# An adaLN block with fast weights and experts: own places for the rows of expert blocks, and another order of the engines at the boundary between two chunks of the scan

## The reference

```python
h = LN(x) * (1 + ca) + sa
x = x + ga * attn(h)            # test-time training with fast weights
h = LN(x) * (1 + cb) + sb
x = x + gb * ffn(h)             # top 2 of 8 experts, with LoRA
```

```python
gate, hb = ki @ w0, ki @ w2;  sg = silu(gate);  hidden = sg * hb
dh = vi @ w1.T;  dhbm = dh * sg;  dgba = silu_backprop(dh * hb, gate)
w1 += NS(einsum(hidden * lr1, vi));  w0 += NS(einsum(ki * lr0, dgba));  w2 += NS(einsum(ki * lr2, dhbm))
w = w / (norm(w) + 1e-5) * norm(w at the start)     # each of the three
o = (silu(qi @ w0) * (qi @ w2)) @ w1
```

## Time and profile before

| | before |
|---|---|
| median of 3 runs | 896.85 us (895.22 to 898.75) |
| profiled execution | 899.54 us, span 897.8 us |
| PE busy | 833.9 us, 93% |
| DVE busy | 687.4 us, 77% |
| ACT busy | 649.2 us, 72% |
| POOL busy | 350.4 us, 39% |
| mean granted clock | 0.984 |

### The profile page before, as it was taken

The page is one execution under the profiler, slowest core; times in us unless marked ns, Lnnn a source line. Parts: engine busy times, 40 slices in busy tenths (PEclk is TensorE's granted clock), DMA queues, the critical chain, the costliest instruction groups (busy, mean ns, idle before and its releaser), DMA issues.

```text
span 897.8 us, 16374 instructions
## 1 busy us (share of the span) xinstructions
PE 833.9 (93%) x4972; PEld 514.8 (57%) x4972; DVE 687.4 (77%) x2354; ACT 649.2 (72%) x1417; POOL 350.4 (39%) x324
## 2 busy tenths in 40 slices
PE   6999999999999999999999999998799999999994
PEld 3647576675757667575766757575555444444441
DVE  2798989898898989889898988989686554454441
ACT  2878988888888889889898988987485434444441
POOL 2324344444544444453444445344114232222222
PEclk9999999999999999999999999999899999999998
DMA  9776435161633517154251614438615465555450
GB/s 326 270 223 178 111 103 154 62 199 46 180 102 112 149 64 213 51 163 109 81 140 51 189 44 100 107 119 251 181 28 93 79 127 93 94 95 86 79 92 4
DMA packets 79126, 111.01 MB, mean 124 GB/s; under 512 B 14128, under 2 KB 35760, under 8 KB 78400
## 3 DMA queue, kind: packets, MB, share of 16 engines
q1 hardware_dynamic: 70720, 92.85, 36.7%
q0 software_dynamic: 8176, 16.85, 9.9%
q10 hardware_dynamic: 144, 0.26, 0.1%
HBM read 47.22 MB, written 64.55 MB: 124 GB/s over the span
## 4 chain that ended last, share of the span: by engine, by line
PE 63%; DVE 15%; ACT 8%; DMA 6%; issue 4%; POOL 3%; SPq 0%; DVEq 0%; POOLq 0%; ACTq 0%
PE bank L129 17%; PE bank L135 7%; PE bank L1060 7%; DMA out_x<-t_arena,t_tokx 4%; PE bank L1070 4%; POOL t_small L2871 2%; PE bank L613 2%; DVE t_small L1549 2%; PE bank L709 2%; ACT t_arena L2481 2%; PE bank L650 1%; PE bank L618 1%; PE bank L645 1%; PE bank L636 1%; DMA xs_scratch<-t_arena 1%
## 5 line engine op out<-in xcount | busy, mean ns | idle before, releaser
L129 PEld LDWEIGHTS bank<-t_arena 128*128 128x128 bf16 (+1 forms) x1536 | 123.2, 122 | 111.4 <-issue 30.5
L129 PE MATMUL bank<-t_arena 128*128 128x128 bf16 (+1 forms) x1536 | 156.1, 236 | 13.0 <-ACT t_arena L2490 6.4
L1060 PE MATMUL bank<-t_arena 128*128 x208 | 93.6, 593 | 0.0
L135 PE MATMUL bank<-t_ident,t_arena 128*128 128x128 f32 x398 | 65.5, 280 | 11.7 <-DVE t_arena L1105 6.2
L3027 POOL DMA_INDIRECT out_x<-t_arena,t_tokx x25 | 38.8, 1552 | 93.7 <-DMA out_x<-t_arena,t_tokx 77.3
L135 PEld LDWEIGHTS bank<-t_ident,t_arena 128*128 128x128 f32 x398 | 46.1, 142 | 45.6 <-issue 17.3
L2798 ACT ACTIVATE t_arena<-t_arena,t_small 128x128 f32<-128x128 f32 x100 | 41.1, 481 | 35.4 <-DVE t_tokx L2191 35.4
L2877 POOL TENSOR_TENSOR t_small<-t_small,t_half 128x8 f32<-128x8 f32 x14 | 24.5, 1748 | 103.5 <-DVE t_small L1549 103.5
L1060 PEld LDWEIGHTS bank<-t_arena 128*128 128x128 f32 x208 | 37.5, 190 | 37.3 <-issue 37.3
L129 PE MATMUL bank<-t_W,t_arena 128*128 128x128 f32 x384 | 54.8, 288 | 0.6 <-ACT t_W L2389 0.2
L1070 PE MATMUL bank<-t_arena 128*128 x108 | 50.8, 593 | 0.5 <-ACT t_arena L2793 0.5
(11 more groups left out here) (1121 smaller groups left out, 2406.9 us busy)
## 6 DMA issues: line engine op xcount, KB each, us to landing
xs_scratch<-t_arena SPq DMA_DIRECT2D x16, 2064.0 KB
t_arena<-xs_scratch SPq DMA_DIRECT2D x156, 64.0 KB
t_arena<-in_gate_up SPq DMA_DIRECT2D x32, 256.0 KB, 3.9
wm_scratch<-t_arena SPq DMA_DIRECT2D x30, 256.0 KB
t_arena<-in_wmod SPq DMA_DIRECT2D x5, 1024.0 KB, 10.4
t_arena<-in_down SPq DMA_DIRECT2D x16, 256.0 KB, 3.1
out_x<-t_arena SPq DMA_DIRECT2D x16, 256.0 KB, 2.1
t_arena<-wm_scratch SPq DMA_DIRECT2D x4, 1024.0 KB
```

Source lines behind the costliest of these rows:

```text
L129: mm = pe.matmul(bank[:, s], lhs[:, s], rhs[:, s], start=True, stop=True)
L135: mm = pe.transpose(bank[:, 128 * k:128 * k + 128], src[:, 128 * k:128 * k + 128], idn)
L1060: mm = pe.matmul(AA(u)[:, :], xT[u % 2][:, 128 * k:128 * k + 128], w_e[:, bass.ds(which[u], 1), 512 * k:512 * k + 512], start=(k == 0), st ...
```

## The change

Two parts in one kernel.

**A, the boundary.** On PE, raw1, raw2, raw0 are turned into B0, B2, B1, the expert-weight matmuls (step `mg`, still L709 in the new numbering) stand ahead of the logits, of raw0's transposes and of the turning of W, which goes W2, W0, W1; the rank matmuls stand behind all of them. On DVE the router's steps from lgc to msk stand behind the scaling of WT1; the merges of chunk c are in the next pass: u0 behind bn_aggr, u1 behind dgb, u2 behind the cast of n2's norm. On ACT kl0 stands between tg and the copy of hb, vl between tm and the cast of G2, both in the next pass; the copies of W go W2, W0, W1. PE has two new waits for merges (u1 before the first matmul into P1, u2 before the first into P2). Chunks 0 and 14 are changed in the same way.

**B, the rows.** Every block's rows, weight and token numbers have a place of their own among 29 (the later blocks take the places of the first again), each block a semaphore `s_g[b]` of its own; `mark` and `s_is` are gone.

```diff
@@ PE, chunk c
                 mm.then_inc(rate_pe, 1)
+                pe.wait_ge(mg_dve, nth(MG_DVE, p-2, "u1"))
                 pe.matmul(P1[:, :], hT[p % 2][:, 0:128], wqkv[1][:, 0, :], start=True, stop=False)
...
+                pe.wait_ge(mg_dve, nth(MG_DVE, p-2, "u2"))
                 pe.matmul(P2[:, :], hT[p % 2][:, 0:128], wqkv[0][:, 0, :], start=True, stop=False)
...
-                turned(pe, P1, raw[1], 4, ident[:, :]).then_inc(prep_pe, 1)
+                pe.wait_ge(n0_act, nth(N0_ACT, c, "ZT1"))
+                turned(pe, B0, raw[1], 4, ident[:, :]).then_inc(prep_pe, 1)
...
-                turned(pe, P2, raw[2], 4, ident[:, :]).then_inc(prep_pe, 1)
...
-                turned(pe, P0, raw[0], 4, ident[:, :]).then_inc(prep_pe, 1)
-                pe.wait_ge(prep_act, nth(PREP_ACT, min(c + 1, NC - 1), "kT"))
-                pe.wait_ge(prep_act, nth(PREP_ACT, min(c + 1, NC - 1), "qT"))
+                pe.wait_ge(n2_act, nth(N2_ACT, c, "ZT1"))
+                turned(pe, B2, raw[2], 4, ident[:, :]).then_inc(prep_pe, 1)
+                pe.wait_ge(mg_dve, nth(MG_DVE, c-1, "u0"))
                 pe.wait_ge(mg_dve, nth(MG_DVE, c-1, "u2"))
                 for j, (e, k) in enumerate(UNITS[c]):
...
                 mm.then_inc(mg_pe, 1)
+                pe.wait_ge(apply_act, nth(APPLY_ACT, a, "lgT"))
+                pe.matmul(A0[:, 0:NE], lgT[:, :], selr[:, 0:NE], start=True, stop=True).then_inc(apply_pe, 1)
...
+                turned(pe, B1, raw[0], 4, ident[:, :]).then_inc(prep_pe, 1)
+                pe.wait_ge(n2_dve, nth(N2_DVE, c, "WT"))
+                pe.wait_ge(prep_act, nth(PREP_ACT, p, "vT"))
+                turned(pe, B2, WT[2], 4, ident[:, :]).then_inc(n2_pe, 1)
                 pe.wait_ge(n0_dve, nth(N0_DVE, c, "WT"))
+                pe.wait_ge(prep_act, nth(PREP_ACT, p, "kT"))
                 turned(pe, B0, WT[0], 4, ident[:, :]).then_inc(n0_pe, 1)
-                pe.wait_ge(n2_dve, nth(N2_DVE, c, "WT"))
-                turned(pe, B2, WT[2], 4, ident[:, :]).then_inc(n2_pe, 1)
+                pe.wait_ge(n1_dve, nth(N1_DVE, c, "WT"))
+                pe.wait_ge(prep_act, nth(PREP_ACT, p, "qT"))
+                turned(pe, B1, WT[1], 4, ident[:, :]).then_inc(n1_pe, 1)
                 pe.wait_ge(apply_dve, nth(APPLY_DVE, a, "msk"))
...
@@ SP, reads of the blocks' rows
-            sp.wait_ge(s_sa, 16)
-            sp.wait_ge(s_is, 2)
-            at = sp.value_load(row0u[0:1, 6:6 + 1], min_val=0, max_val=2048 * NE - 128)
-            rows_in(sp, 6, at)
...
+            for t in range(NB):
+                if t == RING + 4:
+                    store_x1(NC - 2)
...
+                if t >= SLOTS:
+                    sp.wait_ge(s_sa, 16 * (t - SLOTS + 1))
+                at = sp.value_load(row0u[0:1, t:t + 1], min_val=0, max_val=2048 * NE - 128)
+                rows_in(sp, t, at)
```

More of the change, by code:

```diff
@@ L250, in adaln_block @@
         xT = cut(26624, 512, 2)
-        mark = arena[0:1, 28160:28160 + NB]
         def AA(u):
@@ L2383, in _ @@
             row.then_inc(prep_act, 1)
-            for h in range(H):
-                s = slice(128 * h, 128 * h + 128)
-                row = act.activation(kl0[1][:, s], raw[1][:, s], ACT.Identity, scale=lr12[1][:, 0 + h:1 + h])
-            row.then_inc(prep_act, 1)
             act.wait_ge(n0_pe, nth(N0_PE, 0, "TW"))
@@ L2565, in _ @@
             act.activation(tg, B0[:, :], ACT.Tanh, scale=0.5).then_inc(fwd_act, 1)
+            act.wait_ge(rate_dve, nth(RATE_DVE, NC - 1, "lr"))
+            act.wait_ge(prep_dve, nth(PREP_DVE, NC - 1, "tk"))
+            act.wait_ge(n0_pe, nth(N0_PE, NC - 3, "G"))
+            for h in range(H):
+                s = slice(128 * h, 128 * h + 128)
+                row = act.activation(kl0[1][:, s], raw[1][:, s], ACT.Identity, scale=lr12[1][:, 0 + h:1 + h])
+            row.then_inc(prep_act, 1)
             act.wait_ge(fwd_pe, nth(FWD_PE, NC - 1, "hb"))
```

432 lines of the change are left out of this document (192 added, 240 removed).

## The result

The changed kernel took 918.62 us (median of 4 runs, 917.91 to 920.77) against 896.84 us for the kernel before: the ratio is 1.0253, with a 95% interval of 1.0233 to 1.0274. It is slower by 21.8 us.

The account below looks back on a forecast made before the run. PE, busy for 93% of the span, bounds the kernel. 13 periods at +1.50 give 19.5, with +0.8 and +1.2 at the scan's ends and -1.45 at the tail +20.05 us, so 917.0 us; range 898 to 923.

Parts of the forecast that it names:

- The removed wait: PE's 0.90 us wait for qT's copy ahead of L709 goes; gate at best 0.27 us earlier a boundary.
- the copies of W ... are early enough: ACT at the boundary: copies in order W2, W0, W1, without kl0, come early enough for the 0.27 us gain.
- The rank wait: Rank matmuls directly ahead of the gate wait for DVE's msk: gate 0.54 us later (bounds -0.27 to +0.84).
- The reading of the Trainium skill's page: DVE's six router steps go at the pitch of independent operations, so the gate would gain 0.27 us; the prediction doubted it.
- kl0: On ACT, kl0 ahead of the copy of hb delays G2: 0.47 us a chunk (bounds 0 to 1.18).
- The merges: u0, u1, u2 in DVE's dense stretch of the next chunk: +0.49 us a chunk (bounds 0 to 1.83).
- 0.49 more than at G2: PE at the rate matmuls behind n1's norm sum: some 1.50 us late, 0.49 more than G2's 1.01.
- The period: One chunk of the scan: 39.05 + 0.54 + 0.47 + 0.49 = 40.55 us, +1.50.
- Rival 4: PE's boundary waits bring four or five more chunks with a lowered clock, adding 5 to 6 us: 923; chance 0.08.
- The ends: Scan's ends: into chunk 1 +0.8 us in all, including -0.4 for W0's copy; into chunk 15 +1.2 us.
- The tail: Program's end: scatters without reads beside them go from 5.76 to 3.55 us a step, gaining 1.45 us (bounds 0 to -2.4).
- the one sign of being wrong: Program's end: the prediction is wrong if scatters stay 5.7 us apart until the last block.

Follow-up runs that it names:

- e11: Kernel before with the raw tiles turned into the B banks and nothing else: 896.34 us, ratio 1.0007.
- e9: Changed kernel with logits, rank matmuls and DVE's steps lgc to msk at their places in the kernel before: 909.42 us, ratio 1.0118.
- e8: Kernel before with raw tiles turned into the B banks, kl0 behind W1's copy and vl behind the next chunk's tm: 897.56 us, ratio 1.0026.
- e12: e8 with W2 turned ahead of W0 on PE and copied in that order on ACT: 893.40 us, ratio 0.9973.
- e10: e9 with the three merges back at the boundary as well: 896.83 us, ratio 1.0003 to the kernel before.
- e5: Changed kernel with kl0 behind the copy of hb on ACT instead of ahead of it: 924.04 us, ratio 1.0305.
- e3: Changed kernel with the rank matmuls moved behind the next chunk's gate: 916.67 us, ratio 1.0246 to the kernel before.
- e4: Changed kernel with the three merges u0, u1, u2 back at the boundary, nothing else: 908.89 us, ratio 1.0166.
- e2: Kernel before with part B alone (29 places, old boundary): 895.55 us, ratio 1.0007.

## Why the prediction was right

The forecast was 917.0 us, the measurement 918.62; the range and the sign held. By its own steps:

- **The removed wait gives nothing** (forecast: at most 0.27 us a boundary). Right in kind: e11 shows the 0.90 us move to the next wait. But the 0.27 us was not to be had in this order: e9, without the late router steps, still has its gate at 1.43 us. The step that failed is "the copies of W ... are early enough": with L709 ahead of raw0's transposes they are not. Where W0's copy is really early (e8, e12) the gain is 0.20.
- **The rank wait** (forecast +0.54): +0.55, e9 against the changed kernel; the gate is 0.59 later in the trace. The six steps took 0.20 us each, and msk was done 1.26 us after lgc started, where the forecast had 1.24 (its terms, 5 x 0.20 + 0.06 + 0.17, add up to 1.23). The reading of the Trainium skill's page (VectorE: DVE Perf Modes, "The DRAIN you can't avoid") by which they would go at the pitch of independent operations is contradicted by these rows, as by the earlier trace rows. It was my reading: what is measured there is eight copies with and without a semaphore after each, not the pitch of small dependent operations.
- **kl0** (forecast +0.47): +0.37, e10 against the kernel before, for kl0 and vl together. The mechanism in the trace is as told (G2 starts 4.02 us after the gate instead of 3.69, 0.33 later), but e5 shows that the fix that this term suggests makes it worse.
- **The merges** (forecast +0.49): +0.77, e10 against e9. The step that was mis-sized is "0.49 more than at G2". At the boundary all 1.83 us of them are hidden (dhm starts 2.13 us after the gate in e9 and in e10 alike); in the stretch 0.77 of them show. The trace has the same by itself: the rate matmuls are 1.74 us late and G2 0.92, 0.82 less, where the forecast had 1.50 and 1.01. The sum for n1 was forecast 9.51 us after the gate and stands there; it is G2 that was less late, and L613 that comes 0.16 us later than told.
- **The period** (forecast +1.50): 0.55 + 0.77 + 0.37 = 1.69, measured 1.69. The three add up only when they are taken away in this order; e3 and e4 alone give 0.36 each, and together they give -0.19, so 0.54 and 0.49 were never prices of edits to be made one at a time.
- **The long chunks** were a surprise in the other direction: 13 x 1.69 = 22.0, but the 13 steps grew by 18.7 us in the profiles, since 3.2 us of long chunks went away. Rival 4 had expected more of them. Of the 3.2, 2.6 are two lowered clocks and 0.6 one wait for POOL (last section).
- **The ends.** Into chunk 1 the gate came 0.3 us earlier against the set-up's transposes, close to the -0.4 told; the merges that I added to it there (+0.8 in all) were already in the first of the 13 periods, counted twice. From chunk 14's SiLU to the first scatter-add it is 3.2 us more (84.89 to 88.10) where the forecast had 1.2; 0.9 of it is the lower clock behind the count.
- **The tail** (forecast -1.45): 0, by e2 and by the trace. The failing step is "scatters then have no reads beside them, which brings a step to 3.55 us". The short steps of the earlier trace rows were blocks without tokens. I read a difference off two rows without asking what else differed between them. This is also the one sign of being wrong that the prediction named and that came true: the scatters stay about 5.7 us apart until the last block with tokens.

That the sum came within 1.7 us is in part luck. Against it: 13 x 0.19 = 2.5 us of period, 2.0 into chunk 15, and the tail of 1.45. For it: 3.2 us of long chunks, and 1.1 into chunk 1. These sizes come from one profiled execution of each kernel. The same two also differ by 2.9 us less in the set-up and 2.5 us more between the first and the last scatter-add, which nearly cancel; I count neither as the change's, since the first SiLU stands anywhere from 70.2 to 75.1 us in the profiles, and that stretch takes 217.3 to 220.6 us in those of the complete kernels.

## What to carry to other kernels

When a wait is taken away, follow the engine to its next wait and price only the difference; here 0.90 us of idle time was worth nothing, because the next wait was for a chain on another engine that the edit didn't touch. Work moved out of a boundary "into the next stage" is paid in full where an engine has no gap there, and the gap it left is only worth something if somebody else was waiting. Before reading a cost off two instances of the same instruction, check what they moved: a scatter with all its indices out of bounds looks like a fast one. And when a small gain is lost in some passes of a loop and not in others, look for two instructions of different engines that start at the same moment; e8 lost its gain in good part to such a pair.
